# Layer 1's features: one write per tile, and the three-part stack put together on the way back

## What is computed

```python
q = (x @ Wq + bq).reshape(B, S, 16, 8);  k and v likewise
r = (x @ Wr + br).reshape(B, S, 16, 32)
q = concatenate([q, r]);  k = concatenate([k, r])          # 40 features a head
scores = einsum('bqhd,bkhd->bhqk', q / sqrt(40), k)
out = einsum('bhqk,bkhd->bqhd', softmax(scores), v) @ Wo + bo
```

## Time and profile before

| | us |
|---|---|
| median of 3 runs | 1642.0 (1638.96 to 1644.62) |
| profiled execution | 1644.09 |
| its span | 1642.4 |
| PE busy | 1430.6 |
| DVE busy | 1189.8 |
| ACT busy | 1080.1 |
| POOL busy | 729.7 |

### The profile page before, as it was taken

One profiled execution on the slowest core, in us unless ns is written; L12 is line 12 of the kernel. 1 busy time (PEld: TensorE's weight loads), 2 busy tenths in 40 slices (PEclk: granted clock), 3 DMA queues, 4 the chain that ended last, 5 costly groups with the idle time before them and its releaser, 6 DMA issues.

```text
span 1642.4 us, 27700 instructions
## 1 busy us (share of the span) xinstructions
PE 1430.6 (87%) x9478; PEld 626.9 (38%) x9528; DVE 1189.8 (72%) x2067; ACT 1080.1 (66%) x1811; POOL 729.7 (44%) x794
## 2 busy tenths in 40 slices
PE   4599999999999998889888888899899887999846
PEld 2223333335653332355532223244344322545236
DVE  4477778777768878756786788977688889667424
ACT  2166666676556776676677777777687877777712
POOL 5310244334424663477856533354754600656213
PEclk9799999999999999899999999999999999999959
DMA  6745444775733343876312120551320204542022
GB/s 176 240 113 139 121 134 136 223 230 151 249 115 79 96 139 113 247 230 183 114 35 59 33 65 20 188 167 59 107 70 21 72 21 137 170 125 92 1 97 80
DMA packets 127281, 199.06 MB, mean 121 GB/s; under 512 B 16967, under 2 KB 94564, under 8 KB 127142
## 3 DMA queue, kind: packets, MB, share of 16 engines
q1 hardware_dynamic: 120182, 184.32, 37.9%
q0 software_dynamic: 6240, 12.71, 2.3%
q10 hardware_dynamic: 720, 0.26, 0.1%
HBM read 125.65 MB, written 73.46 MB: 121 GB/s over the span
## 4 chain that ended last, share of the span: by engine, by line
PE 66%; DVE 11%; ACT 6%; DMA 5%; issue 5%; POOL 3%; SPq 2%; another core or an unknown queue 0%; ACTq 0%; POOLq 0%; DVEq 0%
PE ps L1133 19%; PE ps L1099 12%; PE ps L1120 11%; DVE Mb L1461 7%; PE ps L1217 5%; ACT P L1309 5%; PE ps L1230 5%; PE ps L1067 4%; PE ps L1141 2%; PE ps L1228 1%; POOL ROW L1375 1%; DMA X<-xs 1%; PE ps L1167 1%; PE ps L1083 1%; PE ps L1186 1%
## 5 line engine op out<-in xcount | busy, mean ns | idle before, releaser
L1461 DVE TENSOR_REDUCE Mb<-ps 128x2 f32<-128x1024 f32 (+1 forms) x955 | 940.8, 1011 | 326.7 <-PE ps L1099 308.8
L1309 ACT ACTIVATE P<-ps 128x1024 f32<-128x1024 f32 (+1 forms) x1065 | 807.0, 787 | 341.8 <-PE ps L1120 329.8
L1120 PE MATMUL ps<-STK 32*128 32x512 f16 (+1 forms) x1536 | 414.5, 388 | 63.5 <-ACT P L1309 27.7
L1099 PE MATMUL ps<-STK 32*128 32x512 f16 (+1 forms) x1536 | 405.2, 387 | 45.0 <-DVE Mb L1461 16.1
L1133 PE MATMUL ps<-P,V 128*32 128x512 f32 x3072 | 417.2, 616 | 8.1 <-ACT P L1309 6.1
L1099 PEld LDWEIGHTS ps<-STK 32*128 32x128 f16 (+1 forms) x1536 | 101.6, 93 | 302.2 <-issue 102.9
L1120 PEld LDWEIGHTS ps<-STK 32*128 32x128 f16 (+1 forms) x1536 | 104.8, 93 | 273.5 <-ACT P L1309 85.0
L1729 POOL DMA_INDIRECT xs<-ROW,slot x64 | 63.7, 996 | 122.9 <-DVE slot L1551 107.8
L1736 POOL TENSOR_TENSOR TH<-TH,Z 128x512 f32<-128x512 f32 x65 | 82.6, 1272 | 74.4 <-ACT Z L1355 73.4
L1217 PE MATMUL ps<-XT,WE 128*128 128x128 f32 x752 | 99.9, 276 | 9.2 <-issue 5.5
L1133 PEld LDWEIGHTS ps<-P,V 128*32 128x32 f32 x3072 | 60.7, 108 | 121.1 <-issue 98.2
(11 more groups left out here) (169 smaller groups left out, 1502.3 us busy)
## 6 DMA issues: line engine op xcount, KB each, us to landing
WE<-in_we SPq DMA_DIRECT2D x94, 576.0 KB
STK<-qka SPq DMA_DIRECT2D x64, 480.0 KB
qka<-HL SPq DMA_DIRECT2D x96, 256.0 KB
STK<-qkb SPq DMA_DIRECT2D x64, 256.0 KB
qkb<-HL SPq DMA_DIRECT2D x96, 128.0 KB
X<-xs SPq DMA_DIRECT2D x84, 129.5 KB
xs<-pad SPq DMA_DIRECT2D x8, 1036.0 KB, 7.6
qka<-HL SPq DMA_DIRECT2D x48, 128.0 KB
```

The source lines that it names most:

```text
L1099: mm = eng.matmul(ps[:, bank + i, :], l_, r_, start=True, stop=True)
L1120: mm = eng.matmul(ps[:, bank + i, :], l_, r_, start=True, stop=True)
L1309: eng.activation(P[:, st % 3, j:j + n, :], ps[:, bank:bank + n, :], ACT.Exp, scale=SCALE_A if g < 4 * B else SCALE_B).then_inc(sem("exp"), 1)
L1461: eng.tensor_reduce(Mb[:, g % 2, at:at + 4 * n - 3:4], ps[:, bank:bank + n, :], AX, ALU.max).then_inc(sem("mx"), 1)
```

## The change

Every tile of layer 1, q, k or r, is now written by one transfer of 256 KB: high and low, 128 rows each, once, into `qka[x]` of form [2, 128, 512]. `stack(g)` makes the three parts as it reads: for each side, the r tile of the group (32 partitions a part) and the 32 rows of q or k that belong to the group (8 partitions a part). For side 0 the high part is read twice and the low once; for side 1 high and low, then high again. That makes 8 transfers a group in place of 2, of 64, 32, 16 and 8 partitions. The bytes that arrive in `STK` are the same, 960 KB, with the parts in another order of rows. The counts that the semaphores are compared with follow (`tp_count`, `pw_count`), and the planner is told: `put` of layer 1 costs 0.6, `stack` 3.6 in layer 1 and 0.4 in layer 2.

```diff
+def pw_count(n):
+    return 16 * (n // HLN + 1) if n < NA * B else 16 * (NA * B // HLN) + 48 * ((n - NA * B) // HLN + 1)
...
-            yield from do(g - 3.4, "stack", g)
+            yield from do(g - 3.4, "stack", g, us=3.6 if g < 4 * B else 0.4)
...
-            yield from do(rank, "put", n)
+            yield from do(rank, "put", n, us=0.6)
...
-        qka = [nc.dram_tensor(f"qka{i}", [4, 960, 512], F16, kind="Internal").ap() for i in range(2)]
+        qka = [nc.dram_tensor(f"qka{i}", [NA, 2, 128, 512], F16, kind="Internal").ap() for i in range(2)]
...
-                            on.wait_ge(f"tp{sl}", 32 * (b - 1))
-                    to = qka[b % 2]
-                    if x < 2:
-                        for o in range(3):
-                            at = (384, 864)[x] + 32 * o
-                            eng.dma_start(to[:, at:at + 32, :], lo if o == 2 - x else hi).then_inc(done, 16)
-                    else:
-                        high = HL[:, i, 0:1, :].broadcast_to([128, 2, 512])
-                        eng.dma_start(to[x - 2, 0:256, :].rearrange("(o r) n -> r o n", o=2), high).then_inc(done, 16)
-                        eng.dma_start(to[x - 2, 480:864, :].rearrange("(o r) n -> r o n", o=3)[:, 0:3:2, :], high).then_inc(done, 16)
-                        low = HL[:, i, 1:2, :].broadcast_to([128, 2, 512])
-                        eng.dma_start(to[x - 2, 256:960, :].rearrange("(o r) n -> r o n", o=2)[0:128], low).then_inc(done, 16)
+                            on.wait_ge(f"tp{sl}", 128 * (b - 1))
+                    eng.dma_start(qka[b % 2][x].rearrange("o r n -> r o n"), HL[:, i, :, :]).then_inc(done, 16)
...
                 for n in needs(g):
-                    on.wait_ge(f"pw{n % HLN}", 48 * (n // HLN + 1))
+                    on.wait_ge(f"pw{n % HLN}", pw_count(n))
                 if b < B:
                     for w in range(2):
-                        eng.dma_start(SA[0:120, sl, w].rearrange("p j n -> p (j n)"),
-                                      qka[b % 2][gl, 480 * w:480 * w + 480, :].rearrange("(p j) n -> p (j n)", j=4)).then_inc(
-                            sem(f"tp{sl}"), 16)
+                        to, done = SA[:, sl, w].rearrange("p j n -> p (j n)"), sem(f"tp{sl}")
+                        for at, c, src in ((0, 32, qka[b % 2][2 + gl]), (96, 8, qka[b % 2][w][:, 32 * gl:32 * gl + 32, :])):
+                            part_of = src.rearrange("o (p j) n -> o p (j n)", j=4)
+                            two_ = part_of[0:1].broadcast_to([2, c, 2048]) if w == 0 else part_of
+                            eng.dma_start(to[at:at + 2 * c, :], two_).then_inc(done, 16)
+                            eng.dma_start(to[at + 2 * c:at + 3 * c, :], part_of[1 - w]).then_inc(done, 16)
```

More of the change, by code:

```diff
@@ L111, in tp_count @@
 def tp_count(g):
-    return 32 * (g // 4 + 1) if g < 4 * B else 32 * B + 16 * ((g - 4 * B) // 4 + 1)
+    return 128 * (g // 4 + 1) if g < 4 * B else 128 * B + 16 * ((g - 4 * B) // 4 + 1)
+def pw_count(n):
+    return 16 * (n // HLN + 1) if n < NA * B else 16 * (NA * B // HLN) + 48 * ((n - NA * B) // HLN + 1)
 AT_COUNT = [b + 1 if b < B else B + 2 * (b - B) + 2 for b in range(NB)]
@@ L906, in put @@
                     for sl in range(4):
-                        on.wait_ge(f"tp{sl}", 32 * B + 32 * (b - 1 - B))
+                        on.wait_ge(f"tp{sl}", 128 * B + 32 * (b - 1 - B))
                 w, s = x // 2, x % 2
@@ L1256, in fhi @@
                     if n >= HLN:
-                        on.wait_ge(f"pw{n % HLN}", 48 * (n // HLN))
+                        on.wait_ge(f"pw{n % HLN}", pw_count(n - HLN))
                     out = HL[:, n % HLN, 0, :]
```

## The result

| | before | after |
|---|---|---|
| median of 4 runs each | 1643.3 us (1639.0 to 1649.8) | 1672.9 us (1671.1 to 1680.7) |
| profiled execution | 1644.1 | 1680.7 |
| its span | 1642.4 | 1679.0 |

After is slower: ratio 1.0187, interval 1.0147 to 1.0228. The forecast was 1637. The time lies inside the range (1617 to 1682), but on the other side of no change.

What follows compares the result with a forecast made beforehand. Layer 1 was taken as bound by PE once it runs and by transfers while it starts. Gains of 2.7 us (start) and 2.0 (steady state) took 1644.1 to 1639.4, 1637 for the median; range 1617 to 1682.

Steps and rivals of the forecast that it cites:

- Two engines for the two-part pieces: Stack pieces with first dimension 2 on the DRAM side run on two DMA engines, 237.6 kB each a group.
- Their rate: The two engines carrying a stack run at 24.3 GB/s each, so a group's stack takes 9.8 us.
- slow bound: Two engines at the present stack's 14.9 GB/s each would take 15.9 us a group.
- The path of the maxima: Steady state, stack issue to maxima landed: 11.6 us, fitting nearly every group with 2 to 3 us to spare.
- The threshold: Stack time a group from which time is lost: 10.9 us at the start, about 13 in steady state.
- rival (c): Puts or weights ahead of stacks cost 3 us in half of 28 groups, or the order wastes that; about 1660; chance 0.08.
- 2 us gained at the batch change: At group 8, behind batch 3's puts, cheaper puts let the maxima land near 167, when PE wants them.
- (a): Two engines run at 15.9 us a group: start loses 22 us, steady state 28; 1692 us; chance 0.20.
- The start: First score at 74.2 instead of 78.4, 4.2 us earlier; less 1.5 us of PE work, 2.7 us gained.
- The new order: Scheduler redraws all engines' order; ACT's 6.4 us more of exponentials costed at nothing to 2 us.
- Rival (b): Stack pieces run over 16 engines: first score near 57, 20 us gained at the start, 2 steadily; 1620 us; chance 0.10.

Runs made afterwards that it cites:

- e1: Changed kernel, but each piece with a two-part source issued as two one-part pieces, eleven a group instead of eight; ratio 0.9736 to the kernel before.
- e5: Changed kernel, but two-part 256 KB piece written to partitions 32 to 95, one-part piece to 0 to 31, 8-row pieces likewise; ratio 1.0042 to the kernel before.
- e3: Changed kernel, but only the two-part 256 KB piece issued as two, nine pieces a group; ratio 0.9807 to the kernel before.
- e6: Changed kernel, but only the two 64 KB two-part pieces issued as two each, ten pieces a group; ratio 0.9990 to the kernel before.
- e2: Kernel before with its own transfers, but the changed kernel's three planner costs, so only the order is new; ratio 0.9879 to the kernel before.
- e4: Changed kernel, but layer 1's row of maxima issued from ACT's queue, right behind the copy that makes it; ratio 1.0079 to the kernel before.
- e7: Changed kernel's transfers with the old planner costs, so in the old order; ratio 1.0370 to the kernel before.

## Why the prediction was wrong, step by step

- **Two engines for the two-part pieces: right.** Share 0.13 for 8.0 us while a stack's rest goes alone, as forecast; e1 takes the tail away by the first dimension alone.
- **Their rate: this step failed.** I had two rates, 24.3 and 14.9 GB/s an engine, and took the first for the whole transfer, since "what slows it looks shared, and two engines alone ask for under 50 GB/s". They are alone for 8.0 of 12.7 us, and there they have 22.5 GB/s each. In the 4.7 us before, the same stack's other pieces keep ten to eleven engines at work, and the two carry 12 GB/s each, less than my slow bound. The term was 9.8 us a group; 12.7 were measured, 2.3 of the difference in those 4.7 us and 0.6 alone. Part of both is the destination (e5): at partitions 32 to 95 the term is 11.0.
- **The path of the maxima: too short by 3.7 us.** I had 1.0 to the first data, 9.8 for the stack and 0.8 for the row's landing, 11.6 us. `stack(4)` is issued at 93.56, its data run from 94.9 to 107.5, and `mput(2)`, issued at 98.07 in the same queue, lands at 108.8, in time for the score at 108.87: 1.3, 12.6 and 1.3, together 15.3, where 14.9 were to be had the earlier trace rows. The rate of the two engines is the term that matters; the two allowances add 0.8.
- **The threshold: right in kind, too high.** "The steady state from about 13", 14 from the first issue: against e3 (8.4 for a lone stack), which loses nothing, e5 and e6 (12.4 and 13.3) lose 18 and 13 us in groups 1 to 31, and after (14.0) 51. An error of 3.7 us in the path was enough to cross it, and the trace showed the engines' rate at both values; 0.62 on the one side was too much.
- **Puts ahead of a stack, rival (c): the mechanism is right, the weight wrong.** I counted 2 us gained at the batch change, from 9 us of issues less. At that very place PE waits 8.8 us, and group 6 takes 25.8 us instead of 17.7. From the issue of `stack(8)`, behind its five puts, to the score it is 17.8 us, where a stack alone takes 15.3. Stacks that travel alone cost little: the waits at 108.87 and 122.54 are 1.05 and 0.71 us. The five longest of the eleven waits are 25.1 of the 31.3 us, and ahead of four of these five stacks SP has puts, padding or weights (the puts ahead of `stack(13)` take 10.4 us to issue, from 231.73). I gave (c) 0.08; it and a tempered (a) are what happened. Its own sum was wrong: 3 us in half of 28 groups, less 5, are 37 us, so about 1679 and not "about 1660".
- **The start: the net is right (2.4 gained, 2.7 forecast), the parts aren't.** The first smax was 4.8 us later than forecast (45.2) and the first score 3.6 (77.8). The new order alone ends group 0 at 83.3 (e2), and with one-part pieces at 71.4 (e1): the two-engine pieces ate 21.7 us there. I saw `mput(0)` move ahead of the puts, and credited it with only what the queue left.
- **The new order: "nothing to 2 us" failed.** It is -20 us (e2). I had valued it by a count of exponentials, and not by the place of the one transfer that PE waits 16 us for the earlier trace rows.
- **The clock wasn't in the sum.** Of the 40.7 us, 12.6 are longer busy time, nearly all of it with a lower granted clock around the new waits.
- **Rival (b)** is what e1 does: first score at 56.2, forecast 57 for that case; 2.6% faster, where I had 1.3% (1620); the order's 1.2%, which the sum had left out, is as large as the difference.

## What to carry to other kernels

Before a transfer is cut or reshaped, look at the first dimension of its access patterns: on the number there hangs how many DMA engines carry it (4 here with a first dimension of 4, 2 with one of 2), and a transfer on two engines delays everything small that follows in its queue. Where a forecast rests on a rate that the trace shows at two values, work out which neighbours are active in each part of the transfer, the transfer's own other pieces included, and check how far the result lies from the threshold. And if a change touches a planner's costs, run the order apart from the rest: here it was worth 20 us, as much as the edit it came with.

## What the runs showed of the hardware

- The rate of a DMA engine depends on where it writes: the two-part piece at partitions 32 to 95 instead of 0 to 63 took a stack from 14.0 to 12.4 us, with the same engines and bytes (e5). With two engines alone it is 25 GB/s each there, and 19.5 (e6) to 22.5 (after) at 0 to 63. Why they have only 12 beside the stack's other pieces isn't shown; no kernel here varied it by itself.
- A single issue on SP can block: L921 takes 4.90 us at 34.26 and 4.53 at 58.54, against a usual 0.6, each time with an earlier stack still on the two engines. In e1, with the same order, the four stacks' issues take 4.6 to 5.0 us in all instead of up to 9.9.
- Waits on PE cost more than their length: in groups 6 to 21 the mean granted clock is 0.94 where it was 0.99 (the two levels are 1.2 and 2.4 GHz), after stalls of up to 8.8 us. In e1 and e3, without these waits, it is 1.00 over groups 1 to 31, in e4 and e7, with them, 0.97.
